# Adding a residual by an identity matmul in the first 16 of 96 chunks, and moving three steps of ScalarE and one DMA of the sync queue

## The reference, cut to what matters

```
x = x + L0(gn(x))     # gn: group norm, 16 groups of 2 channels
x = x + L1(gn(x))

def L0(x):            # deformable convolution
    off = (sigmoid(conv2d(x, w_off, b_off)) - 0.5) * 2       # an x and a y shift for each pixel, in (-1, 1)
    sampled = bilinear sample of x at (pixel - off), mirrored at the borders
    return conv2d(sampled, w_dcn, b_dcn)                      # 3x3, 32 -> 32 channels
def L1(x):            # 3x3 depthwise convolution whose taps come from the image
    kernels = relu(mean(x) @ w1 + b1) @ w2 + b2
    return depthwise(x, kernels)
```

## Time and profile before

| | us |
|---|---|
| median of 3 runs | 1569.52 |
| lowest, highest | 1569.38, 1572.87 |
| the profiled execution | 1571.72 |
| its span in the trace | 1569.8 |
| TensorE busy | 1486.5 (95%) |
| VectorE busy | 1361.0 (87%) |
| ScalarE busy | 1049.1 (67%) |

### The profile page before, as it was taken

One profiled execution on the slowest core, in us unless ns is written; L12 is line 12 of the kernel. 1 busy time (PEld: TensorE's weight loads), 2 busy tenths in 40 slices (PEclk: granted clock), 3 DMA queues, 4 the chain that ended last, 5 costly groups with the idle time before them and its releaser, 6 DMA issues.

```text
span 1569.8 us, 28833 instructions
## 1 busy us (share of the span) xinstructions
PE 1486.5 (95%) x11472; PEld 643.4 (41%) x11472; DVE 1361.0 (87%) x1264; ACT 1049.1 (67%) x1594; POOL 352.9 (22%) x394
## 2 busy tenths in 40 slices
PE   2788989999999999999999999999999999999998
PEld 1333333444444444444444444444444444444443
DVE  3899989999999989899889999999989999999940
ACT  4766557766678667776587766877577766656533
POOL 5000320305031141313303051220503123040010
PEclk9899999999999999999999999999999999999999
DMA  7364445666676657666576757676576856656468
GB/s 254 112 189 151 142 130 186 194 193 207 186 235 210 213 176 227 212 222 209 170 232 204 235 164 213 210 234 205 166 231 195 246 182 197 181 179 198 135 181 257
DMA packets 226726, 308.61 MB, mean 197 GB/s; under 512 B 17056, under 2 KB 168992, under 8 KB 226592
## 3 DMA queue, kind: packets, MB, share of 16 engines
q1 hardware_dynamic: 225040, 305.22, 63.2%
q0 software_dynamic: 1552, 1.55, 0.3%
HBM read 190.28 MB, written 38.14 MB: 146 GB/s over the span
## 4 chain that ended last, share of the span: by engine, by line
PE 48%; DVE 25%; ACT 10%; DMA 7%; issue 5%; SPq 3%; POOL 1%; DVEq 0%; ACTq 0%; POOLq 0%
PE z L400 22%; PE dc L440 13%; PE dw L473 8%; DMA st<-in_planes 6%; DVE nb L809 4%; DVE nb L812 4%; DVE nb L814 4%; PE z L473 3%; DVE xv L799 2%; DVE nb L818 2%; DVE nb L816 2%; DVE nb L800 2%; DVE yr L835 2%; ACT dv L602 2%; ACT mv L609 2%
## 5 line engine op out<-in xcount | busy, mean ns | idle before, releaser
L400 PE MATMUL z<-xv,wos 128*64 128x384 f32 x4608 | 765.2, 488 | 13.9 <-ACT du L602 11.2
L400 PEld LDWEIGHTS z<-xv,wos 128*64 128x64 f32 x4608 | 341.0, 137 | 420.9 <-issue 394.2
L440 PE MATMUL dc<-sr,wds 128*32 128x384 f32 x2304 | 431.1, 520 | 32.4 <-DVE yr L835 30.7
L440 PE MATMUL dc<-sh,wds 128*32 128x384 f32 x2304 | 431.3, 521 | 0.0
L792 DVE COPY_PREDICATED nb<-mu,xv 128x2280 f32<-128x2280 uint16 x96 | 273.7, 2851 | 31.7 <-ACT mu L609 31.4
L440 PEld LDWEIGHTS dc<-sr,wds 128*32 128x32 f32 x2304 | 135.4, 111 | 279.3 <-issue 279.2
L473 PE MATMUL dw<-yr,wy 128*64 128x388 f32 x616 | 229.8, 494 | 7.3 <-ACT ot L637 7.2
L473 PE MATMUL dw<-yh,wy 128*64 128x388 f32 x616 | 230.3, 495 | 0.0
L623 ACT ACTIVATE nb<-xv 128x2292 f32<-128x2292 f32 x96 | 202.8, 2112 | 2.3 <-POOL xv L931 2.0
L656 ACT ACTIVATE junk<-yr,nmx 128x768 bf16<-128x768 f32 x96 | 89.8, 935 | 152.8 <-DVE yr L835 152.7
L645 ACT ACTIVATE st<-st,npiv 128x1152 f32<-128x1152 f32 x56 | 70.3, 1256 | 161.7 <-DMA st<-in_planes 133.3
(11 more groups left out here) (122 smaller groups left out, 1495.4 us busy)
## 6 DMA issues: line engine op xcount, KB each, us to landing
xv<-in_x SPq DMA_DIRECT2D x272, 384.0 KB, 4.7
yr<-in_xr SPq DMA_DIRECT2D x96, 392.0 KB, 7.1
out<-ot SPq DMA_DIRECT2D x96, 388.0 KB, 5.6
yh<-yr SPq DMA_DIRECT2D x178, 196.0 KB, 5.1
st<-in_planes SPq DMA_DIRECT2D x56, 576.0 KB, 7.0
sh<-sr SPq DMA_DIRECT2D x160, 194.0 KB, 2.8
sh<-sr SPq DMA_DIRECT2D x32, 145.5 KB, 2.5
yr<-in_planes SPq DMA_DIRECT2D x8, 576.0 KB, 10.5
```

What stands on the lines that cost most here:

```text
L400: last = nc.tensor.matmul(acc[m], weights[:, kx, :], view[:, :, kx:kx + W], start=kx == 0, stop=kx == 2)
L440: last = nc.tensor.matmul(dc[m, q, 0:NB * PAIRS], weights[:, kx, q], view[:, :, cols], start=first, stop=final)
```

## The change

In chunks 0 to 15 (`LIFTED` = 16) the first half of the deformable convolution no longer has its residual added by VectorE. TensorE adds it in PSUM by four more matmuls with a 128 x 128 identity (a new slice `K_ONE` of the constants), which wait for the residual's DMA, `r_in`, and stand behind the twelve matmuls of that half. ScalarE evacuates the half by `lift`, an Identity with bias that also accumulates the sum, and VectorE skips it. `y_done` becomes one semaphore for each half. For all 96 chunks `y_square` (with `y_totals`) moves behind the second `finish`, and `x_sums` and `x_totals` run one iteration later; `residual` is issued ahead of `st_load`.

```
 def deform(n, q):
-                wait(pe, y_done, Q * (n - 1) + q + 1)
+                wait(pe, y_done[q], n)
+                lifted = q == 0 and n < LIFTED
...
+                if lifted:
+                    pe.wait_ge(r_in[n % YS], ring(n, YS, r_dmas))
+                    at = y_at(n)
+                    for g in range(G):
+                        m = slice(C * g, C * g + C)
+                        last = nc.tensor.matmul(dc[m, q, 0:NB * PAIRS], kc[:, K_ONE][:, m],
+                                                yr[:, at:at + NB, q, 1:PAIRS + 1], start=False, stop=True)
                 last.then_inc(dcn_mm, 1)
 # sync queue
+                if 0 <= i - DCN_STEP:
+                    residual(i - DCN_STEP)
                 if b + 1 < B and o < STILES:
                     st_load(b + 1, o)
-                if 0 <= i - DCN_STEP:
-                    residual(i - DCN_STEP)
 # ScalarE
+            def lift(n):
+                b, j = divmod(n, CHUNKS)
+                k = y_at(n)
+                act.wait_ge(dcn_mm, Q * n + 1)
+                nc.scalar.activation(yr[:, k:k + NB, 0, 1:PAIRS + 1],
+                                     dc[:, 0, 0:NB * PAIRS].rearrange("p (k w) -> p k w", w=PAIRS), ACT.Identity,
+                                     bias=db[b % 2][:, 0:1], accum_out=ys1[b % 2][:, 0, j:j + 1]).then_inc(y_done[0], 1)
...
-                if b + 1 < B and 0 < o <= STILES:
-                    x_sums(b + 1, o - 1)
+                if b + 1 < B and 1 < o <= STILES + 1:
+                    x_sums(b + 1, o - 2)
...
                 side(i, 0)
-                if e >= 0:
-                    y_square(e)
...
                     finish(c, 1)
+                if 0 <= e + 1 < LIFTED:
+                    lift(e + 1)
+                if e >= 0:
+                    y_square(e)
 # VectorE, evacuate(n)
                 for q in range(Q):
+                    if q == 0 and n < LIFTED:
+                        continue
```

More of the change, by code:

```diff
@@ L53 @@
 K_SIGN = slice(P + CQ + TAPS, P + CQ + TAPS + 1)
-K_ALL = P + CQ + TAPS + 1
+K_ONE = slice(P + CQ + TAPS + 1, P + CQ + TAPS + 1 + P)
+K_ALL = P + CQ + TAPS + 1 + P
 M_LOC, V_LOC, M_REL, V_SQ, M_SQ, DEV, DEV_SQ, V_ALL, V_EPS, D_STD = (
@@ L64 @@
 LERPS = 7
+LIFTED = DW_STEP - DCN_STEP
 PADDED = 4
@@ L220, in block_kernel @@
         dcn_mm = sem("dcn_mm")
-        y_done = sem("y_done")
+        y_done = [sem(f"y_done{q}") for q in range(Q)]
         y_sq = sem("y_sq")
@@ L438, in deform @@
                             first, final = kx == 0, kx == 2
-                            final = final and (r == 0 or j < CHUNKS - 1)
+                            final = final and (r == 0 or j < CHUNKS - 1) and not lifted
                             last = nc.tensor.matmul(dc[m, q, 0:NB * PAIRS], weights[:, kx, q], view[:, :, cols],
@@ L449, in deform @@
                             last = nc.tensor.matmul(dc[m, q, n3:n3 + PAIRS], wde[:, kx, q],
-                                                    fe[:, b % 2, kx + h:kx + h + W - 1:2], start=False, stop=kx == 2)
+                                                    fe[:, b % 2, kx + h:kx + h + W - 1:2], start=False, stop=kx == 2 and not lifted)
+                if lifted:
[5 more added lines that the diff above has]
+                                                yr[:, at:at + NB, q, 1:PAIRS + 1], start=False, stop=True)
                 last.then_inc(dcn_mm, 1)
@@ L653, in y_square @@
                 k = y_at(n)
-                act.wait_ge(y_done, Q * (n + 1))
+                for q in range(Q):
+                    act.wait_ge(y_done[q], n + 1)
                 wait(act, y_sq, n)
@@ L720, in _ @@
                 c, e = i - DW_STEP, i - DCN_STEP - 1
-                if b + 1 < B and 0 < o <= STILES:
-                    x_sums(b + 1, o - 1)
-                    if o == STILES:
+                if b + 1 < B and 1 < o <= STILES + 1:
+                    x_sums(b + 1, o - 2)
+                    if o == STILES + 1:
                         x_totals(b + 1)
@@ L744, in _ @@
                 side(i, 0)
-                if e >= 0:
-                    y_square(e)
-                if b and o == 3:
-                    y_totals(b - 1)
                 size(i, 0)
@@ L754, in _ @@
                     finish(c, 1)
+                if 0 <= e + 1 < LIFTED:
+                    lift(e + 1)
+                if e >= 0:
+                    y_square(e)
+                if b and o == 3:
+                    y_totals(b - 1)
                 if i + 1 < TOTAL:
@@ L837, in evacuate @@
                         scalar=db[b % 2][:, q:q + 1], in1=y, op0=ALU.add, op1=ALU.add,
-                        accum_out=ys1[b % 2][:, q, j:j + 1]).then_inc(y_done, 1)
+                        accum_out=ys1[b % 2][:, q, j:j + 1]).then_inc(y_done[q], 1)
             dve.wait_ge(cleared, 3)
@@ L1084 @@
     consts = np.zeros((P, K_ALL), np.float32)
+    consts[:, K_ONE] = np.eye(P)
     consts[:, K_SIGN] = np.where((p // C == 0) | (p // C == G - 1), 1, -1)[:, None]
```

## The result

| kernel | median us | of runs |
|---|---|---|
| before | 1570.92 | 4 |
| after | 1601.78 | 4 |

The ratio is 1.0197, 95% interval 1.0179 to 1.0214: slower by 30.9 us, clear of noise. The forecast was +21.3 (1590.8, range 1574 to 1606). The profiled execution of the changed kernel has a span of 1599.6 us, 29.8 more than that of before.

What follows compares the result with a forecast made beforehand. The prediction took VectorE to bound the first stage and TensorE nearly all of the second. Its terms, -2 + 17.1 + 9 + 7.2 - 10 = +21.3 us on a median of 1569.52, gave 1590.8, range 1574 to 1606.

Steps and rivals of the forecast that it cites:

- the wait of the identity group for `yr<-in_xr`: First stage, TensorE: identity matmuls would wait some 3 to 5 us for the residual's DMA in half of the chunks.
- the turns of 14 and 18 to 20 us: First stage, VectorE: chunk spacing would alternate between about 14 and 18 to 20 us, up to 340 us.
- the fallen clock: First stage, TensorE: the mean clock would fall below 0.94.
- the second stage at its floor: TensorE from the offsets of chunk 19 to the last offsets: about 1158 us instead of 1168.
- Start, -2: Chunk 2: VectorE's 1.96 us wait for `mu` behind `x_sums` would go, -2 us.
- Seven pairs, +17.1: First stage, blends of chunks 2 to 16: seven two-chunk loops of 32.6 us, 228.2 against 211.1, +17.1 us.
- the clock, +9: First stage: six of seven TensorE pauses followed by half clock, 1.5 us each, +9 us, bounds 0 and 14.
- Into the second stage, +7.2: Chunk 17's blend to chunk 19's offsets: chunk 15's residual must land first, +8 less 0.8 for a fast chunk, +7.2 us.
- Second stage, -10: TensorE from chunk 19's offsets: idle from statistics tiles and `mv` waits would go, between 7.3 and 12.6 us, -10.
- terms 1 and 5: The start, -2 us from the `mu` wait at chunk 2, and the second stage, -10 us from TensorE's idle.
- the fast one: First stage: the rival that the residual does not hold TensorE and VectorE sets the pace; 1536 us, chance 0.07.
- The third: First stage: the rival that ScalarE, standing at `lift` with `sides` queued behind, becomes the longer way; 1596 to 1605, chance 0.10.

Runs made afterwards that it cites:

- the last kernel with them: Changed kernel plus 16 unused matmuls ahead of the residual wait in even chunks 0 to 14, and ScalarE's neighbour copy ahead of `lift`: 1593.08 us, ratio 1.0132.

## Why the prediction was right, and where its sizes were off

The direction and the mechanism held at nearly every point that was named: the wait of the identity group for `yr<-in_xr`, the turns of 14 and 18 to 20 us, the fallen clock, the second stage at its floor. Two signs were too small: the wait in half of the chunks is 4.6 to 7.2 us (12.2 once) and not 3 to 5, and the offsets of chunk 19 start 42.6 us later and not some 31. The time lies inside the range and 11 us above the forecast, 8.5 of it in the spans. By its terms, with what the trace gives:

1. *Start, -2.* The blend of chunk 2 ends at 78.36 instead of 80.82: -2.5.
2. *Seven pairs, +17.1, and the clock, +9: together +26.1.* Measured +31.7: the blend of chunk 16 ends at 321.09, 242.7 us after that of chunk 2, where it was 211.1. The landing was sized right (9.5 and 0.1 for the wait taken; 9.3 on the mean of these seven). The clock was too small: all pauses ended in the half clock, not six of seven, and each cost 1.9 us on the path, not 1.5, since the price was read from a row in which only part of the deformable matmuls was slow (mean clock 0.70 over the 5.7 us from 231.3). That is 13 for seven instead of 9. The rest, about half a us a pair, is what I left out of the loop: the small statistics matmuls between the second half and the offsets and the border masks of the first and last chunk of an image (both in the chain above).
3. *Into the second stage, +7.2.* Measured +13.4, from the blend of chunk 16 to the offsets of chunk 19, 35.25 us against 21.88. This term failed in kind and not only in size: I let VectorE go on by itself from chunk 16 to 17 in 14.3 us. It did not, it waited 6.2 us at the last step of that blend for the deformable part of chunk 14, which stood behind a pause and had the 16 tap matmuls in its midst, 3.5 us of them in the chain at that clock. I had named what is queued behind the residual's wait only as the offsets. The range was made of landings and slow stretches and had no room for this wait; that the time fell inside it all the same is in part luck.
4. *Second stage, -10.* Measured -11.2, and -1.6 in the tail. The floor of 1155.5, added up from the chain's rows, is 1.4 under what four kernels reach.

Their sum is -2.5 + 31.7 + 13.4 - 11.2 - 1.6 = 29.8, the difference of the spans. The experiments bear out the parts: 54 us of loss for the lifting as it stands, of which the late residual is all (with the early one lifting gains 10.4), and 25 us of gain from the order, near the 24 of terms 1 and 5 and 16 waits for `mv` of 0.75 us.

Of the rivals, the fast one came true to 1.5 us once its condition was made, so its pricing was sound and its low chance too. The third, ScalarE's longer way, did not set the changed kernel's time: in the eight slow chunks ScalarE was done early and stood 0.5 to 5.5 us for TensorE's offsets ahead of `du`. With the clock held it set the pace in one chunk.

One reading of the first paragraph was off without effect: TensorE's waits for the evacuation go down to 0.5 us in the trace of before, not to 1.1.

## What to carry to other kernels

Moving an addition to another engine also moves the moment at which its operand must be there: find the issue of that operand's DMA in the trace, and what releases it, before counting the cycles saved. Here the same matmuls lost 54 us or gained 10 by one iteration in the issue order. When a stage is near balance between engines, a wait put into the middle of an in-order queue can close a loop over DMA, TensorE, ScalarE and VectorE, as it did here, and the pause can cost again as a slow clock behind it, here 1.9 us each time.

## What the runs showed of the hardware

- In the changed kernel TensorE's eight waits of 4.6 us or more for a residual were each followed by the half clock, the eight of 1.5 us or less never (granted clock 1.00 over the 3 us behind). Between them both happened: in the kernel with the residual ahead of the x loads a wait of 2.87 us was followed by a mean clock of 0.69 over 3 us, one of 2.53 us by 1.00. The stretch lies on whatever comes next, here 1.51 for 0.86 us and 3.3 for 2.1 us.
- Work nobody needs keeps the clock up, as the 5.2 us of added matmuls did in seven of eight pauses (granted clock 0.994 over the run against 0.977), but it did not give back the whole loss: in the last kernel with them, in the six pauses where the residual was still what TensorE waited for, the identity group started 0.6 us later behind the blend than in the changed kernel (9.9 against 9.3 on the mean). That was not expected, and its cause stays open.
- The same 392 KB transfer took 4.1 us (median of the issues between 190 and 260 us) from issue to landing ahead of three x loads and 6.2 behind them, on one queue.
